# A deformable-convolution stage with image columns signed along the rows, one y term by ScalarE per unit, and the window spreads all on ScalarE

## The reference

```python
def deform_conv(x, w, b, ow, ob):
    off = conv2d(x, ow, ob).reshape(Bn, K, 2, Hh, Ww)          # K = 9 taps
    cy = iy[None, None, :, None] + dy[None, :, None, None] + off[:, :, 0]
    cx = ix[None, None, None, :] + dx[None, :, None, None] + off[:, :, 1]
    y0, x0 = jnp.floor(cy), jnp.floor(cx)
    wy, wx = cy - y0, cx - x0
    samp = gather(y0, x0, (1 - wy) * (1 - wx)) + gather(y0, x0 + 1, (1 - wy) * wx) \
         + gather(y0 + 1, x0, wy * (1 - wx)) + gather(y0 + 1, x0 + 1, wy * wx)
    return jnp.einsum('bckhw,ock->bohw', samp, w.reshape(O, Cin, K)) + b[None, :, None, None]
```

## Time and profile before

| | |
|---|---|
| median of 3 runs | 738.11 us (736.78 to 740.56) |
| profiled execution | 740.86 us, span of its instructions 739.0 us |
| PE / DVE / ACT busy | 588.6 / 611.8 / 487.3 us (80% / 83% / 66%) |
| POOL busy | 147.1 us (20%) |
| sampling of the first layer | about 240 to 391 us |
| sampling of the second layer | about 484 to 636 us |

### The profile page before, as it was taken

The page is one execution under the profiler, slowest core; times in us unless marked ns, Lnnn a source line. Parts: engine busy times, 40 slices in busy tenths (PEclk is TensorE's granted clock), DMA queues, the critical chain, the costliest instruction groups (busy, mean ns, idle before and its releaser), DMA issues.

```text
span 739.0 us, 29144 instructions
## 1 busy us (share of the span) xinstructions
PE 588.6 (80%) x13258; PEld 418.5 (57%) x13258; DVE 611.8 (83%) x805; ACT 487.3 (66%) x739; POOL 147.1 (20%) x258
## 2 busy tenths in 40 slices
PE   2719999999887688898885888759988888749491
PEld 1205887765554466665664545348666666628270
DVE  6998999932469999999997533999999999975866
ACT  2776775233029899999993412789999999451514
POOL 1004000010341333433200044033244420000000
PEclk9959999999999899999999898989999999969696
DMA  5004000000778898888710077779888873000003
GB/s 211 0 16 100 4 4 20 4 4 20 190 252 340 256 311 272 272 268 287 250 67 2 3 192 257 314 238 290 277 267 259 256 259 124 4 1 4 2 4 114
DMA packets 30198, 111.16 MB, mean 150 GB/s; under 512 B 11140, under 2 KB 15940, under 8 KB 25976
## 3 DMA queue, kind: packets, MB, share of 16 engines
q0 software_dynamic: 14912, 87.85, 35.7%
q1 hardware_dynamic: 15160, 21.42, 9.6%
HBM read 92.25 MB, written 19.65 MB: 151 GB/s over the span
## 4 chain that ended last, share of the span: by engine, by line
PE 40%; DVE 34%; ACT 12%; issue 7%; DMA 4%; SPq 2%; POOL 0%; DVEq 0%; ACTq 0%
PE psum L1426 11%; PE psum L1514 7%; DVE arena L812 6%; DVE arena L813 6%; PE psum L1480 6%; PE psum L1635 6%; DVE arena L814 5%; DVE arena L806 3%; ACT arena L1222 3%; ACT arena L1221 2%; ACT arena L1232 2%; ACT arena L1212 2%; DMA arena<-offsets_by_batch 2%; PE psum L1444 2%; PE psum L1538 2%
## 5 line engine op out<-in xcount | busy, mean ns | idle before, releaser
L1514 PE MATMUL psum<-arena 64*64 64x297 f32 (+4 forms) x4512 | 231.0, 351 | 46.0 <-DVE arena L814 32.2
L1514 PEld LDWEIGHTS psum<-arena 64*64 64x64 f32 x4512 | 174.4, 140 | 110.3 <-DVE arena L814 56.0
L1730 POOL DMA_DIRECT2D arena<-offsets_by_batch x128 | 79.1, 632 | 208.7 <-DVE arena L814 137.3
L1480 PE MATMUL psum<-arena 32*32 32x512 f32 x2304 | 90.3, 662 | 24.9 <-issue 19.1
L812 DVE SCALAR_TENSOR_TENSOR arena<-arena 128x792 f32<-128x792 f32 (+3 forms) x96 | 92.4, 963 | 3.6 <-ACT arena L1222 2.2
L1232 ACT ACTIVATE arena<-psum 128x792 f32<-128x792 f32 (+1 forms) x96 | 82.8, 862 | 17.3 <-PE psum L1519 8.6
L1426 PE MATMUL psum<-arena 32*32 32x512 f32 x2592 | 93.6, 597 | 0.0
L814 DVE SCALAR_TENSOR_TENSOR arena<-arena 128x792 f32<-128x792 f32 (+3 forms) x96 | 92.2, 960 | 0.0
L813 DVE SCALAR_TENSOR_TENSOR arena<-arena 128x792 f32<-128x792 f32 (+3 forms) x96 | 92.2, 960 | 0.0
L1480 PEld LDWEIGHTS psum<-arena 32*32 32x32 f32 x2304 | 50.4, 107 | 61.7 <-issue 47.3
L1222 ACT ACTIVATE arena<-arena 128x792 f32<-128x792 f32 (+3 forms) x96 | 84.6, 881 | 0.0
(11 more groups left out here) (168 smaller groups left out, 696.8 us busy)
## 6 DMA issues: line engine op xcount, KB each, us to landing
arena<-offsets_by_batch POOLq DMA_DIRECT2D x112, 576.0 KB, 7.9
arena<-offsets_by_batch POOLq DMA_DIRECT2D x16, 624.0 KB, 7.5
offsets<-arena SPq DMA_DIRECT2D x32, 256.0 KB, 9.7
offsets_by_batch<-offsets SPq DMA_DIRECT2D x184, 24.0 KB
arena<-columns POOLq DMA_DIRECT2D x24, 160.0 KB, 9.8
columns<-arena POOLq DMA_DIRECT2D x8, 320.0 KB, 6.8
arena<-in_x SPq DMA_DIRECT2D x4, 512.0 KB, 5.4
out<-arena SPq DMA_DIRECT2D x8, 256.0 KB, 2.2
```

Source lines behind the costliest of these rows:

```text
L1480: ins = t_.matmul(ps_q(2 * axis + h, conv_bank(m) + i), cols(W_CONV[L] + (axis * K + t) * Q, Q, Q * i, Q), ap(XA + (BLK * m + 8 * h + t // ...
L1514: ins = t_.matmul(ps_t(s, bank + r, first * K * w, many * K * w), window, ap(g_at(unit, d0) + first * TW + s * w, [[GS + TW, many], [SLOTS ...
```

## The change

1. `turned_rows`: `copy_columns` takes a group of four image rows in two instructions: rows 0 and 3 of the group unchanged, rows 1 and 2 multiplied by -1.
2. With the signs in the image rows, the product for the row above can be max(y, 0) times the tent (which is kept negative), straight from the loaded offsets. `y_terms` on ACT makes the absolute value alone. DVE's product for the middle row needs one sign on even slots and the other on odd ones, and is made in two halves of 18 rows, the odd half with the subtraction reversed. `copy_samples` evacuates a unit in two halves, the second multiplied by -1.
3. From batch 2 on, all four spreads of a batch are ACT's; DVE spreads for batches 0 and 1 only. The waits on `s_zv` are changed to match.
4. At the edge batches (0 and 15) the middle product and the absolute value are made for 36 rows instead of 39.

```diff
+        def turned_rows(g_, r, step):
+            return (ap(XT + (4 * g_ + r) * C, [[step * C, 2], [H // 2 * C, B], [1, C]]),
+                    ap_ps(g_, [[step * P, 2], [C, B], [1, C]], r * P))
@@ DVE
             def copy_columns(L, g_):
-                v.tensor_copy(ap(XT + 4 * g_ * C, [[C, 4], [H // 2 * C, B], [1, C]]),
-                              ap_ps(g_, [[P, 4], [C, B], [1, C]])).then_inc(s_xtv, 1)
+                v.tensor_copy(*turned_rows(g_, 0, 3))
+                v.tensor_scalar(*turned_rows(g_, 1, 1), -1.0, None, ALU.mult).then_inc(s_xtv, 1)
...
                     dve.wait_ge(s_nd, UNITS * L + unit + 1)
-                    v.scalar_tensor_tensor(term(0), term(0), 0.0, part(tx), ALU.min, ALU.mult)
-                    v.scalar_tensor_tensor(term(1), term(1), 1.0, part(tx), ALU.subtract, ALU.mult)
+                    for odd in range(2):
+                        own = ap(g_at(unit, 1) + odd * TW, [[2 * TW, KR // 2], [1, 2 * WB[u]]])
+                        v.scalar_tensor_tensor(own, own, 1.0, ap(tx + odd * W + u * TW, [[2 * W, KR // 2], [1, 2 * WB[u]]]),
+                                               ALU.subtract, ALU.mult, reverse0=(odd == 1))
+                    v.scalar_tensor_tensor(term(0), part(ty), 0.0, part(tx), ALU.max, ALU.mult)
                     v.scalar_tensor_tensor(term(2), part(ty), 0.0, part(tx), ALU.min, ALU.mult).then_inc(s_g, 1)
-                    if u == 1 and 1 <= n < NB - 1:
-                        spread_windows(L, n + 1)
@@ ACT
             def copy_columns(L, g_):
-                a.activation(ap(XT + 4 * g_ * C, [[C, 4], [H // 2 * C, B], [1, C]]),
-                             ap_ps(g_, [[P, 4], [C, B], [1, C]]), ACT.Copy).then_inc(s_xta, 1)
+                a.activation(*turned_rows(g_, 0, 3), ACT.Copy)
+                a.activation(*turned_rows(g_, 1, 1), ACT.Copy, scale=-1.0).then_inc(s_xta, 1)
...
-                    for i in (2, 3):
+                    for i in range(2 if n < 2 else 0, 4):
                         ins = nc.scalar.activation(*spread_views(c, a, b, i), ACT.Copy, scale=con("image4", i, 1))
...
-                a.activation(term(0), part, ACT.Copy, scale=-1.0)
-                a.activation(term(1), part, ACT.Abs).then_inc(s_nd, 1)
+                a.activation(ap(g_at(unit, 1), [[TW, KR], [1, 2 * WB[u]]]),
+                             ap(in_at(n, 1) + u * TW, [[W, KR], [1, 2 * WB[u]]]), ACT.Abs).then_inc(s_nd, 1)
...
-                ins = a.activation(ap(SAMP + n // 2 % 2 * SPAR + n % 2 * SLOTS * K * SX + u * WB[0],
-                                      [[SR, 2], [SX, KR], [1, w]]),
-                                   ap_ps(bank, [[CH, 2], [w, KR], [1, w]]), ACT.Copy)
+                to = SAMP + n // 2 % 2 * SPAR + n % 2 * SLOTS * K * SX + u * WB[0]
+                for half, sign in ((0, 1.0), (1, -1.0)):
+                    ins = a.activation(ap(to + half * 2 * K * SX, [[SR, 2], [SX, 2 * K], [1, w]]),
+                                       ap_ps(bank, [[CH, 2], [w, 2 * K], [1, w]], half * 2 * K * w), ACT.Copy, scale=sign)
@@ PE, POOL
-                        pe.wait_ge(s_zv, NB * L + n + 1)
+                        pe.wait_ge(s_zv, 2 * L + min(n + 1, 2))
-                    pool.wait_ge(s_zv, NB * L + 2 * (c - 1))
+                    pool.wait_ge(s_zv, 2 * L + 2)
```

More of the change, by code:

```diff
@@ L1218, in y_terms @@
                     act.wait_ge(s_un, UNITS * L + unit - RING + 1)
-                part = ap(in_at(n, 1) + u * TW, [[W, in_rows(n)], [1, 2 * WB[u]]])
-                term = lambda d: ap(g_at(unit, d), [[TW, in_rows(n)], [1, 2 * WB[u]]])
-                a.activation(term(0), part, ACT.Copy, scale=-1.0)
-                a.activation(term(1), part, ACT.Abs).then_inc(s_nd, 1)
+                a.activation(ap(g_at(unit, 1), [[TW, KR], [1, 2 * WB[u]]]),
+                             ap(in_at(n, 1) + u * TW, [[W, KR], [1, 2 * WB[u]]]), ACT.Abs).then_inc(s_nd, 1)
             def copy_samples(L, unit):
@@ L1231, in copy_samples @@
                 edge = n in (0, NB - 1)
-                ins = a.activation(ap(SAMP + n // 2 % 2 * SPAR + n % 2 * SLOTS * K * SX + u * WB[0],
-                                      [[SR, 2], [SX, KR], [1, w]]),
-                                   ap_ps(bank, [[CH, 2], [w, KR], [1, w]]), ACT.Copy)
+                to = SAMP + n // 2 % 2 * SPAR + n % 2 * SLOTS * K * SX + u * WB[0]
+                for half, sign in ((0, 1.0), (1, -1.0)):
+                    ins = a.activation(ap(to + half * 2 * K * SX, [[SR, 2], [SX, 2 * K], [1, w]]),
+                                       ap_ps(bank, [[CH, 2], [w, 2 * K], [1, w]], half * 2 * K * w), ACT.Copy, scale=sign)
                 if edge:
                     ins = a.activation(ap(SE + u * WB[0], [[3 * SX, 2], [SX, 3], [1, w]]),
-                                       ap_ps(bank, [[CH, 2], [w, 3], [1, w]], KR * w), ACT.Copy)
+                                       ap_ps(bank, [[CH, 2], [w, 3], [1, w]], KR * w), ACT.Copy,
+                                       scale=-1.0 if n == 0 else 1.0)
                 ins.then_inc(s_se, 1)
```

## The result

The changed kernel takes 731.79 us (median of 12 runs, 725.94 to 734.23), the kernel before, run beside it, 736.90 (12 runs, 733.03 to 741.55). The medians lie 5.1 us apart. The ratio that is taken over all runs is 0.9915 with a 95% interval of 0.9889 to 0.9940: faster by 6.3 us, between 4.4 and 8.2. The forecast was 13.6 us and 724.5. The direction came out, the measured time lies inside the range of 719.5 to 733.5, near its slow end, and the gain is less than half of the forecast's. The profiled execution took 729.70 us, its span is 727.5, against 740.86 and 739.0 before.

A forecast was written before the change was run, and what follows sets the result against it. DVE was taken to set the pace, with a round through PE, ACT and DVE as long as the pair in the second layer. 12.4 + 2.2 - 0.8 - 0.2 = 13.6 us off the median 738.11 gives 724.5, range 719.5 to 733.5.

The forecast's parts named there:

- The net of 6.2 a layer: DVE in sampling: 9.1 us saved on spreads less 2.9 for extra half products, 12.4 in both layers.
- the 732: Whole kernel if the halves cost 13.1 us instead of 5.9, by the skill's fixed cost per instruction: near 732.
- the rivals' 728.4 and 733: Second-layer clock still drops: 728.4, chance 0.25; drops in both layers, or in second with extra instructions at 0.12: about 733, 0.16.
- the drop of the clock: PE's clock at half after waits before even units; five further second-layer pairs at 0.78 us more, 728.4, chance 0.25.
- the dear instructions: Extra DVE instructions at 0.12 us instead of 0.07, 4.2 us in all; alone 728.7.
- while PE's own work between stays: PE's wait before even units: DVE gets 0.45 us shorter, PE's work is unchanged, so the wait shrinks from 2.01 to 1.56.
- The 0.8 set aside: One pair at the second layer's start, at dropped clock behind a long wait: 20.02 - 19.24 = 0.8 us lost.
- The sum: Total gain: 12.4 + 2.2 - 0.8 - 0.2 = 13.6 us.
- It is level with DVE and has nothing to spare.: Round ending an odd batch, with row copies: ACT takes 8.2 us and DVE leaves it 8.2.
- the part on what costs nothing: Column copies, POOL's and SP's lists, offset loads and moved waits charged at nothing; a layer's last copy 0.1 us longer.
- the sign against: In the changed kernel's profile, ACT's four spreads stepping over 2.1 us would show the forecast wrong.
- The slower rival: ACT's late copies hold PSUM banks, PE stops inside a batch and a second clock drop follows: 754 us, chance 0.05.

The follow-up runs named there:

- the second execution: The changed kernel run again unaltered: 728.69 us (median of 6) against 737.51 for the kernel before, ratio 0.9885.
- The two best orders: Changed kernel with ACT's four spreads one unit later: 725.41 us, ratio 0.9830; the same with row copies also ahead of distances: 723.19 us, ratio 0.9836.
- the second execution of the kernel before: The kernel before run again unaltered, one execution: 741.47 us, beside a median of 738.05 for 11 others.

## Why the prediction came out as it did

**DVE's load: right.** The spreads were to give 9.1 a layer and cost 9.0 (the run with spreads on both engines). The halves were to cost 2.9 and cost 3.0 (45 of them against whole products of 36 rows). The net of 6.2 a layer was measured as 5.95 and 6.03 in busy time, and as 12.3 in both layers after idle time is taken off.

**The fixed cost of an instruction: the trace was right.** By the Trainium skill ("VectorE: DVE Perf Modes", the section on the TRN2 errata) an instruction cut in two was to cost about 0.16 us more, by the forecast's estimate. In this full queue it costs 0.07, by timeline and by experiment. The page's figure is for one operation by itself and is no price for one more in a row. There was some luck in the 0.07: the two steps in the earlier trace rows differ by 0.08 as they stand, which is 1.11 ns an element and leaves 0.02; the forecast took the low end of what rounding allows. And the 732 that the page's figure would have given lies beside the measured 731.8 by coincidence, since the halves didn't cost that. In the same way the measured time lies between the rivals' 728.4 and 733, and neither the drop of the clock nor the dear instructions came.

**The clock: right.** It was to stay at 1.00 before even units in both layers, and it did: the granted clock is 1.00 from 262.00 to 387.01 and from 492.09 to 624.24. The slow first units are gone, seven in the second layer and two in the first. The wait of PE was to shrink to 1.56 and shrank to 1.79. DVE's part came out: from the odd batch's first unit to the next even one it is 9.42 us (303.42 to 312.84) for 9.87 before, the 0.45 of the forecast. But the step "while PE's own work between stays" was wrong: PE begins its third unit 5.63 us after the first (309.05) where it took 5.80, and samples it in 2.00 instead of 2.06, so 0.23 came back as waiting. The clock held all the same. The 0.8 set aside for one slow pair at the start of the second layer wasn't lost: behind the long wait there the clock is 0.50 (482.67 to 485.00), but DVE waits for nothing before 508.16.

**DVE's waits for y terms: wrong, and this is most of the miss.** The sum took them as gone, 2.2. They were replaced, by others for the y terms and by new ones for row copies: 4.9 us in the stretches (5.9 in the second execution) where the sum had 0.8. That is 4.1 to 5.1 of the 13.6, and the step that failed. The mechanism had been seen and was charged at nothing: "It is level with DVE and has nothing to spare." A round with no slack was counted as a round that fits. It fits as long as nothing in it is late; but the same paragraph took no row on how late loads and PE can be, and the part on what costs nothing said of the offset loads only that "they start sooner when it is sooner". They start sooner and take as long as before (7.6 us from issue to landing in the first layer's stretch before, 7.5 after, medians), while ACT, no longer full, comes to them early. Three things show that lateness on a round without slack was the cause: taking away the source (half the bytes, 4.3 us to land) gives 143.8 to 144.3 a stretch; putting the four spreads behind the first release gives 143.9 and 144.1 in the first layer with late loads still there; and with two of the spreads back on DVE late loads and stops cost DVE nothing.

**ACT: right in load.** Its share of 0.95 at full pace came out at 0.94 (47.08 of 50 us). The spreads step 2.05 for four, under the 2.1 that was named as the sign against. The slower rival, ACT holding PSUM banks, showed as three waits of PE, 1.6 us in all, none with a clock drop behind it.

**What is left.** The traces give 9.4 and 8.6 us less in the stretches (292.8 and 293.6 for 302.3), and the ratios of the times 6.3 (4.4 to 8.2) and 8.5. Execution by execution the changed kernel spreads over 8 us. Sampling isn't all of that: its two traced executions differ by 3.4 us in span, and the shorter one has the longer stretches, so outside them the same instructions took 434.7 and 430.5 us. Differences of that size cover the one between 9.4 and 6.3; where in the program they sit isn't shown. The two best orders, at 0.983 and 0.984, have the 13.6 us of the forecast (0.9815) inside their intervals.

## What to carry to other kernels

Count the slack of each round through several engines and not only the load of each engine: a round that is just as long as the bottleneck's pace passes a late transfer on to it. Put work that nobody waits for soon behind the instruction that releases the bottleneck, even when the engine has room for it. And when a gain comes out short, first see whether the bottleneck's busy time fell as forecast; the rest is then idle time with a releaser, to be followed back to the first thing that was late.

## What the runs showed of the hardware

PE stopped inside sampling without a releaser in the profile, 0.2 to 2.2 us at a time, at a DMA share of about 0.75, and did not in the changed kernel at 0.44 to 0.47. Every one of the 45 stops ended 1.2 to 1.7 us after the end of a 16 KB packet of the instruction queue q8. Behind the one of 2.19 the unit went on slowly (3.42 us for 44 matmuls, granted clock 0.50).

Offset loads that made a full ACT wait 0.2 us in all made one at 88% wait 4.3 in all, up to 1.0 at a time (1.3 in the second execution), although the transfers moved the same bytes at nearly the same share (0.75 and 0.72, 0.76 and 0.74) and took as long to land.

Waits of PE of 1.78 and 1.79 were followed by the full clock each time in the changed kernel (2.4 GHz, a unit of 2.35 or 2.36 us). Waits of 2.01 in the kernel before were followed by it twice in the first layer and by a unit of 3.94 at 354.75. One wait of 1.83 in the second execution of the kernel before was followed by 3.54.
